# Halved slots for pair rows and plane staging in a graph kernel, so that four small units are in flight

## The reference

```python
msgs = edge_vals[:, None] * x[edge_col]               # edge_row = src, edge_col = dst, edge_vals = weights
agg = jax.ops.segment_sum(msgs, edge_row, num_segments=n)
h = (1.0 + eps[0]) * x + agg
h = _bn_relu(h @ W1 + b1, g1, be1)
h = _bn_relu(h @ W2 + b2, g2, be2)
```

## Time and profile before

| | |
|---|---|
| median of 3 runs | 3895.01 us (3892.2 to 3898.1) |
| profiled execution, own time | 3895.72 us |
| its span | 3894.0 us |
| PE busy in the span | 3403.9 us (87%) |
| DVE, ACT, POOL busy | 2366.4, 835.4, 651.0 us |
| pair stage, first and last start of L738 | 269.8 and 892.2 us |
| idle time of PE ahead of L738, for pair rows | 225.7 us in 10 times |

### The profile page before, as it was taken

One profiled execution on the slowest core, in us unless ns is written; L12 is line 12 of the kernel. 1 busy time (PEld: TensorE's weight loads), 2 busy tenths in 40 slices (PEclk: granted clock), 3 DMA queues, 4 the chain that ended last, 5 costly groups with the idle time before them and its releaser, 6 DMA issues. The chain is left out here.

```text
span 3894.0 us, 33669 instructions
## 1 busy us (share of the span) xinstructions
PE 3403.9 (87%) x12468; PEld 1931.2 (50%) x12468; DVE 2366.4 (61%) x3072; ACT 835.4 (21%) x1097; POOL 651.0 (17%) x463
## 2 busy tenths in 40 slices
PE   6989855977999999799826999999999999966998
PEld 6877644764554554345513444444444444454444
DVE  9972211335010211334379988998998899857987
ACT  0103212334000000133202222222222222242222
POOL 3788888830000000000000000000000000011000
PEclk9999978998999999899857999999999999987999
DMA  9989967992444344122254222222322232275222
GB/s 359 363 257 277 259 165 175 278 218 69 137 131 133 123 134 154 43 72 60 79 153 129 63 69 84 72 76 65 94 85 70 84 94 74 75 255 178 65 66 65
DMA packets 263804, 525.88 MB, mean 135 GB/s; under 512 B 91593, under 2 KB 152799, under 8 KB 262111
## 3 DMA queue, kind: packets, MB, share of 16 engines
q1 hardware_dynamic: 149561, 443.29, 36.0%
q10 hardware_dynamic: 52480, 60.01, 5.2%
q0 software_dynamic: 61600, 20.44, 4.9%
HBM read 361.99 MB, written 161.67 MB: 134 GB/s over the span
## 5 line engine op out<-in xcount | busy, mean ns | idle before, releaser
L1010 PE MATMUL ps<-R,B 125*128 125x500 f32 x2800 | 1095.2, 542 | 20.8 <-DVE R L1822 13.4
L1010 PEld LDWEIGHTS ps<-R,B 125*128 125x128 f32 x2800 | 503.9, 190 | 592.2 <-issue 544.7
L614 POOL DMA_INDIRECT pairs<-w x400 | 620.9, 1552 | 196.5 <-issue 140.2
L855 PE MATMUL ps<-R,H 125*128 125x500 f32 (+1 forms) x1400 | 554.2, 553 | 35.0 <-DVE R L1595 21.7
L1208 ACT ACTIVATE R<-R,asc 125x1625 f32<-125x1625 f32 (+1 forms) x200 | 320.2, 1601 | 1079.8 <-DVE R L1809 1079.8
L625 POOL DMA_DIRECT2D B<-ct_d x50 | 27.2, 546 | 2696.9 <-PE ps L1010 2571.9
L1822 DVE SCALAR_TENSOR_TENSOR R<-R 125x1625 f32<-125x1625 f32 (+1 forms) x250 | 444.8, 1779 | 0.0
L1809 DVE SCALAR_TENSOR_TENSOR R<-H,asc 125x1625 f32<-125x1625 f32 (+1 forms) x200 | 368.9, 1845 | 115.3 <-PE ps L1017 87.3
L738 PE MATMUL ps<-R,H 125*128 125x375 f32 (+1 forms) x1000 | 314.5, 463 | 117.8 <-DMA R<-pairs 117.8
L855 PEld LDWEIGHTS ps<-R,H 125*128 125x128 f32 x1400 | 258.8, 195 | 316.3 <-issue 313.7
L1684 DVE SCALAR_TENSOR_TENSOR Fb<-R,asc,Fb 125x1625 f32<-125x1625 uint16 (+1 forms) x192 | 353.7, 1842 | 5.5 <-DVE Fb L1684 0.5
(11 more groups left out here) (281 smaller groups left out, 2799.4 us busy)
## 6 DMA issues: line engine op xcount, KB each, us to landing
pairs<-R SPq DMA_DIRECT2D x25, 3200.0 KB
R<-ct_d SPq DMA_DIRECT2D x175, 406.2 KB, 3.2
R<-ct_d SPq DMA_DIRECT2D x175, 375.0 KB, 3.1
R<-pairs SPq DMA_DIRECT2D x25, 2500.0 KB
R<-wt_d SPq DMA_DIRECT2D x50, 812.5 KB, 4.4
R<-wt_d SPq DMA_DIRECT2D x50, 750.0 KB, 4.2
wt_d<-R ACTq DMA_DIRECT2D x13, 1250.0 KB
wt_d<-B ACTq DMA_DIRECT2D x12, 1250.0 KB
```

The lines of the kernel that those rows point to most:

```text
L614: pool.indirect_dma_start(pairs, bass.IndirectOffsetOnAxis(ap=key_u[:, c:c + 1], axis=0), val[:, c, :], None, compute_op=ALU.add)\
L855: last = mm(ps[:, bank, at:at + w], rows[0:Q, j, f * 128:(f + 1) * 128], TL[q % TS][0:Q, o:o + w], start=j == 0 and at == 0, stop=j == NB ...
L1010: last = mm(ps[:, bank, at:at + w], rows[0:Q, j, f * 128:(f + 1) * 128], TT[q % TR][0:Q, o:o + w], start=j == 0 and at == 0, stop=j == NB ...
```

## The change

A slot is halved. There are four half slots for the rows and four for the staging, at the same addresses as before in sum. A unit of 4 blocks takes two halves side by side (half slots 0 and 1, or 2 and 3), a unit of 2 blocks or 1 takes one. `slots_of` works out for each unit its first half slot (`SLOT`), how many it takes (`WIDTH`), how many units have begun at that half slot (`COUNT`, for the semaphores), and which units held these half slots before (`PRIOR`). Units 0 to 24 get half slots 0 and 2 by turns, as before; units 25 to 39 get 2, 3, 0, 1, 2, 3 and so on. For units 25 and 26 the prior is 23, for 27 and 28 it is 24, and from 29 on it is i - 4. The semaphores of the two stores become one per half slot, `planes_st`, that counts 32 a unit.

```diff
+def slots_of(units):
+
+    slot, width, count, prior = [], [], [], []
+    at, user, uses = 0, {}, [0] * 4
+    for i, (g, part) in enumerate(units):
+        w = 2 if PG[g][1] > 2 else 1
+        at += at % w
+        first = at % 4
+        mine = range(first, first + w)
+        uses[first] += 1
+        slot.append(first)
+        width.append(w)
+        count.append(uses[first])
+        prior.append(sorted({user[k] for k in mine if k in user}))
+        for k in mine:
+            user[k] = i
+        at = (at + w) % 4
+    return slot, width, count, prior, uses
...
-        PR = [R[:, s * 8 * PW:(s + 1) * 8 * PW].rearrange("p (m n t) -> p m n t", m=4, t=2) for s in range(2)]
+        def pair_rows_at(i):
+
+            s, m = SLOT[i], 2 * WIDTH[i]
+            return R[:, s * 4 * PW:(s + WIDTH[i]) * 4 * PW].rearrange("p (m n t) -> p m n t", m=m, t=2)
...
+        def stage_at(i):
+
+            s, h = divmod(SLOT[i], 2)
+            w = WSTF[s][:, h * 2 * PW:(h + WIDTH[i]) * 2 * PW]
+            c = CSTF[s][:, h * PW:(h + WIDTH[i]) * PW].bitcast(U16)
+            return w.rearrange("p (b c) -> p b c", b=PB), c.rearrange("p (b c) -> p b c", b=PB)
...
-                if i >= 2:
-                    sp.wait_ge(S("l0_pe"), 4 * (i - 1))
-                    sp.wait_ge(S("tr_pe"), PB * (i - 1))
-                    sp.wait_ge(S("deg_done"), i - 1)
-                sp.dma_start(PR[i % 2][:, 0:nb, :, :],
+                if PRIOR[i]:
+                    u = PRIOR[i][-1]
+                    sp.wait_ge(S("l0_pe"), 4 * (u + 1))
+                    sp.wait_ge(S("tr_pe"), PB * (u + 1))
+                    sp.wait_ge(S("deg_done"), u + 1)
+                sp.dma_start(pair_rows_at(i)[:, 0:nb, :, :],
...
-                pe.wait_ge(S(f"prow{i % 2}"), 16 * (i // 2 + 1))
+                pe.wait_ge(S(f"prow{SLOT[i]}"), 16 * COUNT[i])
...
                 act.dma_start(wt_d[bb:bb + PB, :, j0 * Q:(j0 + nb) * Q].rearrange("b p c -> p b c"),
-                              WST[s][:, :, 0:nb * Q]).then_inc(S(f"w_st{s}"), 16)
+                              wst[:, :, 0:nb * Q]).then_inc(S(f"planes_st{SLOT[i]}"), 16)
...
-                if i >= 2:
-                    act.wait_ge(S(f"w_st{s}"), 16 * (i // 2))
-                    act.wait_ge(S(f"c_st{s}"), 16 * (i // 2))
+                for u in PRIOR[i]:
+                    act.wait_ge(S(f"planes_st{SLOT[u]}"), 32 * COUNT[u])
```

More of the change, by code:

```diff
@@ L48 @@
 PUNITS = [(g, part) for g in range(len(SIZES)) for part in range(PARTS)]
+def slots_of(units):
[15 more added lines that the diff above has]
+    return slot, width, count, prior, uses
+SLOT, WIDTH, COUNT, PRIOR, USES = slots_of(PUNITS)
 LAYERS = 6
@@ L131, in gnn_stack @@
         HW = LW // 2 + 1
-        PR = [R[:, s * 8 * PW:(s + 1) * 8 * PW].rearrange("p (m n t) -> p m n t", m=4, t=2) for s in range(2)]
+        def pair_rows_at(i):
+            s, m = SLOT[i], 2 * WIDTH[i]
+            return R[:, s * 4 * PW:(s + WIDTH[i]) * 4 * PW].rearrange("p (m n t) -> p m n t", m=m, t=2)
         WSTF = [R[:, 16 * PW:20 * PW], B[:, 2816:2816 + 4 * PW]]
         CSTF = [PT[:, 0:2 * PW], B[:, 0:2 * PW]]
-        WST = [t.rearrange("p (b c) -> p b c", b=PB) for t in WSTF]
-        CST = [t.bitcast(U16).rearrange("p (b c) -> p b c", b=PB) for t in CSTF]
+        def stage_at(i):
[3 more added lines that the diff above has]
+            return w.rearrange("p (b c) -> p b c", b=PB), c.rearrange("p (b c) -> p b c", b=PB)
         aggL = R[:, 0:2 * LW].rearrange("p (k c) -> p k c", k=KT)
@@ L404, in pair_load @@
                     sp.sem_inc(S("pairs_begun"), 1)
-                if i >= 2:
-                    sp.wait_ge(S("l0_pe"), 4 * (i - 1))
-                    sp.wait_ge(S("tr_pe"), PB * (i - 1))
-                    sp.wait_ge(S("deg_done"), i - 1)
-                sp.dma_start(PR[i % 2][:, 0:nb, :, :],
+                if PRIOR[i]:
[4 more added lines that the diff above has]
+                sp.dma_start(pair_rows_at(i)[:, 0:nb, :, :],
                              pair_rows[j0:j0 + nb, :, part * PW:(part + 1) * PW, :].rearrange("m p c t -> p m c t"))\
-                    .then_inc(S(f"prow{i % 2}"), 16)
+                    .then_inc(S(f"prow{SLOT[i]}"), 16)
             sp.wait_ge(S("merged"), NSC)
@@ L434, in _ @@
             sp.dma_start(w31[:, :, :], W31.rearrange("(k p) n -> p k n", p=128)).then_inc(S("w31_in"), 16)
-            for s in range(2):
-                sp.wait_ge(S(f"w_st{s}"), 16 * (len(PUNITS) // 2))
-                sp.wait_ge(S(f"c_st{s}"), 16 * (len(PUNITS) // 2))
+            for s in range(4):
+                if USES[s]:
+                    sp.wait_ge(S(f"planes_st{s}"), 32 * USES[s])
             for k, a in enumerate((as31, ad31)):
@@ L738, in l0_chunk @@
                         last = mm(ps[:, n % 4, 0:w], H[0:Q, j0 + m, k * 128:(k + 1) * 128],
-                                  PR[i % 2][0:Q, m, o:o + w, 0],
+                                  pair_rows_at(i)[0:Q, m, o:o + w, 0],
                                   start=m == 0, stop=m == nb - 1 and not own, skip_group_check=True)
@@ L758, in plane_block @@
                         last = tr(ps[0:Q, 4 + 2 * (n % 2) + t, m * Q:(m + 1) * Q],
-                                  PR[i % 2][0:Q, m, b * Q:(b + 1) * Q, t], ident[0:Q, 0:Q])
+                                  pair_rows_at(i)[0:Q, m, b * Q:(b + 1) * Q, t], ident[0:Q, 0:Q])
                 last.then_inc(S("tr_pe"), 1)
             for i in range(len(PUNITS)):
-                pe.wait_ge(S(f"prow{i % 2}"), 16 * (i // 2 + 1))
+                pe.wait_ge(S(f"prow{SLOT[i]}"), 16 * COUNT[i])
                 for c, (o, w) in enumerate(LCHUNKS):
@@ L1104, in plane_store @@
                 j0, nb = PG[g]
-                s = i % 2
+                wst, cst = stage_at(i)
                 act.wait_ge(S("tr_ev"), PB * (i + 1))
@@ L1108, in plane_store @@
                 act.dma_start(wt_d[bb:bb + PB, :, j0 * Q:(j0 + nb) * Q].rearrange("b p c -> p b c"),
-                              WST[s][:, :, 0:nb * Q]).then_inc(S(f"w_st{s}"), 16)
+                              wst[:, :, 0:nb * Q]).then_inc(S(f"planes_st{SLOT[i]}"), 16)
                 with nc.allow_non_contiguous_dma(reason="columns of a block"):
                     act.dma_start(ct_d[bb:bb + PB, :, j0 * Q:(j0 + nb) * Q].rearrange("b p c -> p b c"),
-                                  CST[s][:, :, 0:nb * Q]).then_inc(S(f"c_st{s}"), 16)
+                                  cst[:, :, 0:nb * Q]).then_inc(S(f"planes_st{SLOT[i]}"), 16)
             for i, (g, part) in enumerate(PUNITS):
                 nb = PG[g][1]
-                s = i % 2
-                if i >= 2:
-                    act.wait_ge(S(f"w_st{s}"), 16 * (i // 2))
-                    act.wait_ge(S(f"c_st{s}"), 16 * (i // 2))
+                wst, cst = stage_at(i)
+                for u in PRIOR[i]:
+                    act.wait_ge(S(f"planes_st{SLOT[u]}"), 32 * COUNT[u])
                 for b in range(PB):
@@ L1122, in _ @@
                     act.wait_ge(S("tr_pe"), n + 1)
-                    a(WST[s][0:Q, b, 0:nb * Q], ps[0:Q, 4 + 2 * (n % 2), 0:nb * Q], ACT.Copy)
-                    a(CST[s][0:Q, b, 0:nb * Q], ps[0:Q, 5 + 2 * (n % 2), 0:nb * Q], ACT.Copy).then_inc(S("tr_ev"), 1)
+                    a(wst[0:Q, b, 0:nb * Q], ps[0:Q, 4 + 2 * (n % 2), 0:nb * Q], ACT.Copy)
+                    a(cst[0:Q, b, 0:nb * Q], ps[0:Q, 5 + 2 * (n % 2), 0:nb * Q], ACT.Copy).then_inc(S("tr_ev"), 1)
                     if b == 0 and i:
@@ L1428, in _ @@
                 j0, nb = PG[g]
-                rows = PR[i % 2]
-                dve.wait_ge(S(f"prow{i % 2}"), 16 * (i // 2 + 1))
+                rows = pair_rows_at(i)
+                dve.wait_ge(S(f"prow{SLOT[i]}"), 16 * COUNT[i])
                 for m in range(nb):
```

## The result

| | before | changed |
|---|---|---|
| median, first chip | 3895.01 us (7 runs, 3890.3 to 3898.1) | 3877.91 us (7 runs, 3868.87 to 3882.77) |
| ratio, first chip | | 0.9957, 95% interval 0.9946 to 0.9969 |
| ratio, second and third chip | | 0.9948 (0.9935 to 0.9962), 0.9962 (0.9948 to 0.9975) |
| profiled execution, own time | 3895.72 us | 3868.87 us |

The change is faster by 0.4 to 0.5%, 15 to 22 us, on each of three chips. The profiled execution happens to be the fastest of the seven, so its 26.9 us are not all the change's. I therefore read one distance in each profile: from the issue of unit 30's load, just behind the gate, to the first product of the next stage.

The account below looks back on a forecast made before the run. The chain of one staging store at a time bounds the pair stage's small units. Ending that stage at 870, between TensorE's 866.3 and the DMA engines' 871 to 876.3, not 893.7, gives 3895.7 - 23.7 = 3872.0 us, range 3863 to 3888.

Parts of the forecast that it names:

- The bound: Pair stage, small units: a chain of one store at a time, 9.9 and 9.6 us each, makes ScalarE and then TensorE wait.
- Units 25 to 29: TensorE is through at 795.4, not 806.9, but none of these 11.5 us is won by itself, because of the gate.
- Units 30 to 34: Two-block units behind the gate, paced by TensorE unstalled: 4 x 7.36 + 8.24 = 37.7 us.
- The start of unit 30: Gate opens at 798.6, rows take 6.5 us, lost clock 2.0: start at 807.1 (bounds 803.0 and 808.5).
- The clock's price: TensorE's slow first products at unit 30 after some 10 us idle: 2.0 us, 2.3 at most.
- The one-block units: Units 35 to 39, paced by TensorE: 4 x 4.2 + 4.65 = 21.5 us, ending the pair stage at 866.3.
- The account by the DMA engines: Units 30 to 39: 16.8 MB behind the gate in 67.7 us at share 1.08, stage end 871; 876.3 at share 1.0.
- My sign of over 270 GB/s: Sign that the forecast is right: DMA over 270 GB/s in the stretch of units 31 to 34.
- Rival A: DMA engines are full already in the small units, stage ends at 883.7: gain 10.0 us, 3885.7 us; chance 0.15.
- Rival B: Another equal wait, ScalarE's two issues per unit or the last gate, replaces the store's: no gain, 3895 us; chance 0.06.
- Rival C: More loads in flight from 744 us delay the scatters, so the gate at 798.6 slips: slower, 3903 us; chance 0.04.
- the forecast's own bounds: Pair stage ending at 862 to 876, so a total time of 3864 to 3878 us.

Follow-up runs that it names:

- e1: The change with only the staging halved, pair rows again in two whole slots; ratio 0.9977 to the kernel before, distance 81.0 us.
- e2: The change with only the pair rows halved, staging again in two whole slots; ratio 1.0006 to the kernel before, distance 98.2 us.
- e3: The change with the w31 load moved behind the waits for the plane stores; 3866.01 us, ratio 0.9938 to the kernel before.
- e7: The change with w31 later and unit 32's load waiting for unit 30's rows, so two loads go out together at the gate; 3866.22 us, ratio 0.9946.
- e4: The change with the count stores of units 24 to 39 issued by SyncE, which also put w31 late; ratio 0.9942 to the kernel before.
- e6: The change with the count stores of units 24 to 39 issued by SyncE, but w31 early, right behind the last pair rows; ratio 0.9939.
- e11: The change with w31 later and loads spaced, plus 25 filling products on TensorE before unit 30; 3862.59 us, ratio 0.9943.
- e9: The change with w31 behind the plane stores, run again beside the unmodified change on one chip; 3861.96 us, ratio 0.9937 to the kernel before.
- e10: The change itself, unmodified, run a third time on the third chip; 3873.43 us, ratio 0.9962 to the kernel before.
- e8: The change itself, unmodified, run again on the second chip; 3867.18 us, ratio 0.9948 to the kernel before.

## Why the prediction was right, and where its size was off

**The bound** was as told. With the store's wait taken away (e1) 13.4 of the 15.6 to 20.7 us of distance are there, and some half of the gain in time; with only the loads taken out of their wait (e2) there is none. That the early loads feed TensorE behind the gate was in the prediction too, and e1's waits for rows bear it out.

**The size.** Counted from unit 30's load, the forecast is 5.8 for the rows (6.5 from 798.6, which is 0.7 ahead of the load), 2.0 for the clock, 37.7 for units 30 to 34, 21.5 for the one-block units, and 3.7 on top for the DMA engines, together 70.7. The profile has 9.7, 2.6, 37.6, 28.9 and nothing on top, together 78.8.

**Units 25 to 29** are won and given back at the gate: TensorE is idle for 6.97 us before 805.35. **Units 30 to 34** took 845.58 - 805.35 = 40.2 us, of which some 2.6 are the slow start: 37.6 against my 37.7.

**The start of unit 30** was mis-sized by 2 to 4 us: 9.7, 8.0 and 9.2 us from load to start in three profiles, against 5.8. Part of it is a misreading: I added the wait's 12.8 us to the end of the load before and had the gate open at 798.6, but it ended at 799.2, just ahead of the load at 799.33. For the rest, I had a row with one store beside it (7.56) and went below it as for a quieter queue. Whether the three more loads behind the first make it longer is not shown; the start varies from 5.8 to 9.7 us where four go out together. The clock's price was 2.6, where I took 2.0.

**The one-block units** are the term that failed: 874.44 - 845.58 = 28.9 us, not 21.5. In the two other profiles of the change they took 25.0 and 26.0. With w31 later they take 870.18 - 848.40 = 21.8 in e3, and 20.6 to 23.7 in all five such profiles. The step behind it reads "What is late next is TensorE itself, or the DMA engines"; what was late was ScalarE, held up in issuing. I listed what SyncE's loads of pair rows do earlier, and left out the next instruction on the same queue. It was in the code that I read, and costing it would have been short: 1 MB more among stores that then have three units' time to land. I also had a queued load slow a store and not block it; I did not ask what becomes of the next issue. For ScalarE no row of before showed an issue beyond 1.2 us. But the trace of before had the sign on SyncE, in a place that I did not look at: behind the two 2500 KB loads of units 0 and 1 and some loads of weights, two issues took 3.59 and 3.92 us.

```profile
266.43 3.59 SPq L419 DMA_DIRECT2D wA<-in_L_gnn_W  x1
270.06 3.92 SPq L419 DMA_DIRECT2D wB<-in_L_gnn_Wl  x1
```

**The account by the DMA engines** was too high as an upper figure. Unit 39's rows were there in time in e3, at a share of 1.16, above the 1.08 that I had taken. My sign of over 270 GB/s didn't fit my own account: 16.8 MB in 67.7 us are 248 GB/s, and the changed kernel moved 246 in the stretch of units 31 to 34.

**Rival A** is refuted: it has 85 us from the gate to the end, at the rates of before (228 GB/s, then 171). The change takes 73.7 to 78.8, with 246 GB/s in units 31 to 34 and 195 in the one-block units, and the intervals of the ratio lie below A's 0.9974 on the first two chips; on the third the interval just reaches it (0.9975). **Rival B** said that ScalarE's two issues per unit might take the store's place, and I refuted it with their usual length. It was right on the place and wrong on the size: 10.2 us were held up in the profile of the change, and gaps of TensorE of 5.28 and 1.99 us stand behind them. The second of these costs nothing, as TensorE then waits at the gate anyway. **Rival C**: POOL's waits for landings rose from 4.3 to 7.2 us, the longest from 0.3 to 1.0, and unit 30's load went out no later, so nothing of it came. The chances were added up wrong by 0.01: 0.75 + 0.15 - 0.02 is 0.88 for faster, and 0.08 for the same.

In sum the forecast of 23.7 us stands against 17.1 by the medians of the first chip and 22 and 15 on the others. The median of 3877.91 lies at the slow edge of the forecast's own bounds (3864 to 3878), and what brought it there, a held-up issue, is in none of their terms; that it is still inside is in part luck. The version with w31 later reaches 23 and 26 us (3866.01 and 3861.96 against 3888.9 and 3887.97), which is what the forecast described. It beats the kernel before on both chips. It beat the change by 11.5 us on the one chip where both ran; with the loads spaced as well (e7) it was as fast as the change on another, and e4, e6 and e11 are as fast as it within the spread of the runs.

## What stays open

How many rows a queue takes before an issue blocks was not measured, nor what holds up the issues near 768 us and at 803.63 in e9. By the distances of e3 and e9 against the change's, w31 costs 1 to 8 us in the pair stage; e9 and e10 differ by 11.5 us in time, e7 and e8 by 1.0. The spread of single runs is some 10 us, and which of these is nearest is not settled.

## What to carry to other kernels

When a wait on a queue is made shorter, read what stands behind it on this queue to its end: a transfer that was harmless where it was may now start among those that matter. More slots take away the wait for a landed store, but a compute engine that issues its own stores can then be held up in the issue, which the wait view shows under no semaphore and no DMA, but only as "issue"; look for issue rows that take longer than their usual time. A look over the whole trace of before, other stages and other engines too, can show such a row ahead of the change. More loads in flight alone gain nothing while another transfer's landing is the one waited for, and can make that landing later (12.5 us at the longest against 6.9).

## What the runs showed of the hardware

The issue of a store from ScalarE took 0.55 us as a rule and up to 6.18 us when earlier stores of the same queue and large loads were in flight, and ScalarE's copies stood still behind it. When half of these stores went to SyncE's queue (e4, e6), SyncE's issues took up to 5.16 and 4.33 us and ScalarE's stayed under 0.6. In the kernel before SyncE's issue of a weight load took up to 3.92 us behind the loads queued ahead of it. The DMA share held 1.16 with TensorE fed, so a share of 1 is no sign of full engines. TensorE's first eight products behind 6.97 us of idle time took 5.37 us, at a granted clock of 0.50 (1.2 GHz), and 2.80 at 1.00 (2.4 GHz) with other products run in between. They took 5.37 behind 2.97 us of idle time too, and 2.92 behind 2.31 (e1).
